# Dense products of a four-layer kernel: two tiles at a time, 712 columns as seven products of summed blocks

## The reference

```
x = x + x @ W0.T + 2 * sum_e gate_e * (x @ A_e.T) @ B_e.T     # 8 experts of rank 16, the two best by x @ Wr.T + bias
x = x + per batch: weights[condition].T @ x                   # mixes the 64 tokens of a batch
x = x + (x @ B2[adapter].T) @ A2[adapter].T                   # rank 16, one of 64 adapters for each batch
x = x + x @ W3.T + b3 + 2 * (x @ A3[slot]) @ B3[slot]         # rank 16, one of 32 slots for each batch
```

## Time and profile before

| | us |
|---|---|
| median of 3 runs (lowest to highest) | 938.36 (937.98 to 939.08) |
| the profiled execution | 938.59 |
| its span, first to last instruction | 936.8 |
| PE busy | 926.4 (99%) |
| DVE busy | 494.9 (53%) |
| ACT busy | 258.7 (28%) |
| POOL busy | 97.0 (10%) |

### The profile page before, as it was taken

How to read it: one execution, slowest core, us unless ns; L and a number is a source line. 1 busy time by engine, 2 the same in 40 slices (tenths; PEclk the granted TensorE clock), 3 DMA queues, 4 the chain that set the end, 5 groups by cost and what they waited for, 6 DMA issues and landing times.

```text
span 936.8 us, 14565 instructions
## 1 busy us (share of the span) xinstructions
PE 926.4 (99%) x4980; PEld 862.6 (92%) x4980; DVE 494.9 (53%) x1431; ACT 258.7 (28%) x526; POOL 97.0 (10%) x218
## 2 busy tenths in 40 slices
PE   8999999999999999999999999999999999999996
PEld 7888888888888899999999999999999999999996
DVE  6654444444333334565556555565655555565554
ACT  5544333333223222122212222221222122222211
POOL 1000110010000011011101111110111111011110
PEclk9999999999999999999999999999999999999999
DMA  7978776997676424655556465556556564655552
GB/s 246 313 257 267 222 250 220 317 327 224 205 231 188 142 83 115 186 155 163 165 161 177 138 185 154 174 145 179 159 159 168 157 185 131 189 158 166 156 166 94
DMA packets 93788, 175.10 MB, mean 187 GB/s; under 512 B 14609, under 2 KB 56978, under 8 KB 93714
## 3 DMA queue, kind: packets, MB, share of 16 engines
q1 hardware_dynamic: 93714, 174.17, 61.7%
HBM read 130.61 MB, written 49.81 MB: 193 GB/s over the span
## 4 chain that ended last, share of the span: by engine, by line
PE 98%; DMA 1%; DVE 0%; ACT 0%; issue 0%; SPq 0%; DVEq 0%
PE ps_y L886 46%; PE ps_o L861 27%; PE ps_v L861 9%; PE ps_o L898 5%; PE ps_y L892 5%; PE ps_o L985 2%; PE ps_v L922 1%; PE ps_o L958 1%; DMA chunk_a_raw<-mov 1%; PE ps_t L969 1%; PE ps_o L956 1%; PE ps_t L946 0%; PE ps_t L976 0%; PE ps_v L966 0%; DVE outb L846 0%
## 5 line engine op out<-in xcount | busy, mean ns | idle before, releaser
L886 PE MATMUL ps_y<-w_hi,x_hi 128*128 128x408 f32 x768 | 272.8, 355 | 0.0
L886 PE MATMUL ps_y<-w_hi,x_lo 128*128 128x408 f32 x768 | 267.4, 348 | 0.0
L886 PE MATMUL ps_y<-w_lo,x_hi 128*128 128x408 f32 x768 | 266.9, 348 | 0.0
L886 PEld LDWEIGHTS ps_y<-w_hi,x_hi 128*128 128x128 f32 x768 | 146.2, 190 | 1.9 <-issue 0.3
L886 PEld LDWEIGHTS ps_y<-w_hi,x_lo 128*128 128x128 f32 x768 | 144.4, 188 | 0.2
L886 PEld LDWEIGHTS ps_y<-w_lo,x_hi 128*128 128x128 f32 x768 | 144.2, 188 | 0.2
L658 DVE TENSOR_TENSOR stat_lo<-stat_raw,stat_hi 128x1024 fp32r<-128x1024 f32 (+1 forms) x63 | 75.0, 1191 | 24.3 <-ACT stat_hi L537 23.2
L861 PE MATMUL ps_o<-chunk_a_hi,stat_hi 128*128 128x512 f32 x216 | 84.5, 391 | 1.6 <-DVE chunk_a_lo L658 1.6
L861 PE MATMUL ps_o<-chunk_a_lo,stat_hi 128*128 128x512 f32 x216 | 84.1, 389 | 0.0
L861 PE MATMUL ps_o<-chunk_a_hi,stat_lo 128*128 128x512 f32 x216 | 84.0, 389 | 0.0
L658 DVE TENSOR_TENSOR y_lo<-ps_y,y_hi 128x408 fp32r<-128x408 f32 (+1 forms) x96 | 50.6, 536 | 57.1 <-ACT y_hi L537 57.1
(11 more groups left out here) (134 smaller groups left out, 1420.4 us busy)
## 6 DMA issues: line engine op xcount, KB each, us to landing
up<-tu SPq DMA_DIRECT2D x128, 256.0 KB, 5.0
stat_raw<-stat SPq DMA_DIRECT2D x59, 512.0 KB, 4.7
mdraw<-t SPq DMA_DIRECT2D x128, 208.0 KB, 2.9
x_raw<-x SPq DMA_DIRECT2D x32, 512.0 KB, 3.7
out<-outb SPq DMA_DIRECT2D x31, 512.0 KB, 5.1
t<-md_a SPq DMA_DIRECT2D x16, 576.0 KB, 6.8
chunk_a_raw<-mov SPq DMA_DIRECT2D x24, 256.0 KB, 5.8
tu<-rows_hi SPq DMA_DIRECT2D x24, 256.0 KB, 4.4
```

Of the source, the lines that this page charges most:

```text
L886: last = nc.tensor.matmul(ps_y[n][:, 0:YB], xT[par][a][:, k, :], w[c][:, k, Y[n]], start=k == 0 and m == 0, stop=k == KB - 1 and m == len( ...
```

## The change

Tiles are handled in pairs: a = 2j and b = 2j + 1, in 16 steps and one more. The 1024 columns of M are split: 312 (`PL`) stay an ordinary product, and with the 136 and 64 columns of the experts and adapters they make one product of 512 columns for each tile (`plain`, 24 matmuls). The other 712 are two halves of STRASSEN = 356 columns. For them the pair of tiles and M are 2 by 2 blocks: rows are tile a and tile b, inner blocks are the upper and the lower 512 features. Four sums of blocks of x (S1 to S4, made on POOL by `sums` for each pair) and four of M (T1 to T4, made on DVE once, in the last chunk of the table stage) allow seven products instead of eight (`winograd`, 12 matmuls of 356 columns each), in Winograd's form of Strassen's method. The products accumulate in PSUM where the form adds them, and ACT and DVE copy and add the partial results part1 and part2.

With it move: x is loaded a second time for the sums (`load_s2`, `load_s3`, `load_s4`), x and the sums lie in the places of the ring of stationary blocks and of the row buffers of the table stage; `ud_lo` goes from DVE to POOL; the high parts of the stacks go from DVE to ACT; the last chunk of the table stage makes M before the adapters' rows, and each group of rows for tu2 goes to it in four stores instead of two, for its columns now lie in two places. `mixed` waits for all three outputs of the tile before. The order of every engine's step is new. The diff, cut to its core:

```diff
+STRASSEN = 356
...
+    GROUPS += [(3, s) for s in U2_BLOCKS + [B0_BLOCK] + M0_BLOCKS]
+    GROUPS += [(4, s) for s in M0_BY_TWO + [B0_BLOCK] + U2_BLOCKS]
...
+    SH = STRASSEN
+    PL = D - 2 * SH
+    PH = PL // 2
...
+    MD_AT, P_AT, WCOLS = HL, HL + MD, HL + MD + PL
...
+    YE = (0, MD + PL, MD + PL + SH, YCOLS)
...
+            def load_x1(j):
+                if at(j, 0):
+                    sp.wait_ge(pe_group, G - 2)
+                else:
+                    sp.wait_ge(pe_p[3], j)
+                sp.dma_start(x1raw[:, :, :], x[2 * j + 1]).then_inc(ld_x1, 16)
...
+            def load_s3(j):
+                if at(j, 0):
+                    sp.wait_ge(st_rows[0], rows_stored(UNITS - 2))
+                else:
+                    sp.wait_ge(pe_p[6], j)
+                sp.dma_start(Sraw[2], x[2 * j][:, upper, :]).then_inc(ld_s[2], 16)
...
+            def step(j, front, back, fin):
+                a, b, a1, b1, b2 = 2 * j, 2 * j + 1, 2 * j - 2, 2 * j - 1, 2 * j - 3
+                if back:
+                    load_up(a1, chosen2.pop(a1), tu2, up2, pe_up2, ld_up2)
+                if front:
+                    load_md(b)
+                if fin:
+                    store_out(b2)
+                if back:
+                    load_up(a1, chosen3.pop(a1), tu3, up3, pe_out[2], ld_up3)
+                    load_mix(b1)
+                if front and not at(j, PAIRS - 1):
+                    load_x0(j + 1)
+                if back:
+                    load_up(b1, chosen2.pop(b1), tu2, up2, pe_up2, ld_up2)
+                    load_up(b1, chosen3.pop(b1), tu3, up3, pe_out[2], ld_up3)
+                if front and not at(j, PAIRS - 1):
+                    load_s2(j + 1)
+                    load_md(a + 2)
+                    load_s3(j + 1)
+                if back:
+                    store_out(a1)
+                if front and not at(j, 0):
+                    load_mix(a)
+                if front and not at(j, PAIRS - 1):
+                    load_x1(j + 1)
+                    load_s4(j + 1)
...
+            def sums(j):
+                def combine(dst, in0, in1, op):
+                    nc.gpsimd.tensor_tensor(out=dst, in0=in0, in1=in1, op=op).then_inc(pool_s, 1)
+                pool.wait_ge(ld_x1, 16 * (j + 1))
+                if at(j, 0):
+                    pool.wait_ge(pe_group, G - 1)
+                else:
+                    pool.wait_ge(pe_p[4], j)
+                combine(Sraw[0], x1raw[:, upper, :], x1raw[:, lower, :], ALU.add)
+                pool.wait_ge(ld_s[2], 16 * (j + 1))
+                combine(Sraw[2], Sraw[2], x1raw[:, upper, :], ALU.subtract)
+                pool.wait_ge(ld_s[1], 16 * (j + 1))
+                pool.wait_ge(pool_s, 4 * j + 1)
+                combine(Sraw[1], Sraw[0], Sraw[1], ALU.subtract)
+                pool.wait_ge(ld_s[3], 16 * (j + 1))
+                pool.wait_ge(pool_s, 4 * j + 3)
+                combine(Sraw[3], Sraw[3], Sraw[1], ALU.subtract)
...
+                if front:
+                    sums(j)
+                    place_w(b)
+                    ud_lo(b)
+                if back:
+                    mix_identity(b1)
+                if front:
+                    place_b(b)
+                    if not at(j, PAIRS - 1):
+                        place_w(a + 2)
+                        ud_lo(a + 2)
+                        place_b(a + 2)
+                    mix_identity(a)
...
+                        nc.vector.tensor_tensor(out=T3raw[:, n, :], in0=src[:, cols], in1=T3raw[:, n, :], op=ALU.subtract)
+                        dve.wait_ge(dve_t1, 2 * n + 2)
+                        nc.vector.tensor_tensor(out=T2raw[:, n, :], in0=src[:, cols], in1=T1raw[:, n, :],
+                                                op=ALU.subtract).then_inc(dve_ev, 1)
...
+                if front:
+                    x1_lo(j)
+                if back:
+                    h2_lo(a1)
+                if front:
+                    hidden_sum(a)
+                    gate(a)
+                    s_lo(j, 0)
+                    hidden_rows(a)
+                if back:
+                    h3_lo(a1)
+                if front:
+                    s_lo(j, 1)
+                    s_lo(j, 2)
+                if back:
+                    mix_lo(b1)
+                if front:
+                    s_lo(j, 3)
+                    if not at(j, PAIRS - 1):
+                        x0_lo(j + 1)
+                    hgT_lo(a)
+                    gate(b)
+                    plain_lo(a)
+                    hidden_sum(b)
+                if back:
+                    add_bias(a1)
+                if front:
+                    dve.wait_ge(pe_La, j + 1)
+                    dve.wait_ge(act_part, 3 * j + 1)
+                    nc.vector.tensor_tensor(out=yraw[0][:, YL], in0=ps_x[:, 0:SH], in1=part1[:, :],
+                                            op=ALU.add).then_inc(dve_La_raw, 1)
+                    hidden_rows(b)
+                    hgT_lo(b)
+                    dve.wait_ge(act_La, j + 1)
+                    rest(y[0][lo][:, YL], yraw[0][:, YL], y[0][hi][:, YL]).then_inc(dve_La, 1)
...
+            def plain(t, ks):
+                rows = x0 if t % 2 == 0 else x1
...
+                        last = nc.tensor.matmul(plain_bank(t)[:, 0:WCOLS], rows[a][:, k, :], w[c][:, k, :],
+                                                start=k == 0 and m == 0, stop=k == KB - 1 and m == len(PASSES) - 1,
+                                                skip_group_check=True)
...
+            def winograd(ps, rows, weights, first):
+                for k in range(HALF_KB):
+                    for m, (a, c) in enumerate(PASSES):
+                        last = nc.tensor.matmul(ps[:, 0:SH], rows[a][:, k, :], weights[c][:, k, :],
+                                                start=first and k == 0 and m == 0, stop=k == HALF_KB - 1 and m == len(PASSES) - 1,
+                                                skip_group_check=True)
+                return last
...
+                    pe.wait_ge(dve_x0, j + 1)
+                    pe.wait_ge(pool_md, a + 1)
+                    if at(j, 0):
...
+                        pe.wait_ge(dve_ev, M_DONE + 1)
...
+                        pe.wait_ge(dve_yp, b1 + 1)
+                    plain(a, range(0, 3))
+                if fin:
+                    h3_rows(b2)
+                if front:
+                    plain(a, range(3, 5))
+                if fin:
+                    ranks3(b2)
+                if front:
+                    plain(a, range(5, KB)).then_inc(pe_hl, 1)
+                    if at(j, 0):
...
+                    hidden_product(a)
+                if back:
+                    pe.wait_ge(dve_mix, a1 + 1)
+                    pe.wait_ge(dve_yp, a1 + 1)
+                    pe.wait_ge(dve_La, j)
+                    pe.wait_ge(dve_Ra, j)
+                    if fin:
+                        for n in range(3):
+                            pe.wait_ge(dve_out[n], a1)
+                    mixed(a1)
+                if front:
+                    if not at(j, 0):
+                        pe.wait_ge(dve_Lb, j)
+                    winograd(ps_w, A11, B11, True).then_inc(pe_p[0], 1)
+                if back:
+                    if front:
+                        pe.wait_ge(dve_vsum, 2 * a + 2)
+                    pe.wait_ge(dve_h2, a1 + 1)
+                    h2_rows(a1)
+                if front:
+                    if not at(j, 0):
+                        pe.wait_ge(dve_Rb_raw, j)
+                    winograd(ps_x, A12, B21, True).then_inc(pe_p[1], 1)
+                if back:
+                    ranks2(a1)
+                if front:
+                    repeated(a)
+                    pe.wait_ge(dve_x1, j + 1)
+                    pe.wait_ge(pool_md, b + 1)
+                    if not at(j, 0):
+                        pe.wait_ge(dve_Ra_raw, j)
+                    plain(b, range(0, HALF_KB))
+                if front:
+                    pe.wait_ge(dve_udb, a + 1)
+                if back:
+                    h3_rows(a1)
+                if front:
+                    plain(b, range(HALF_KB, KB)).then_inc(pe_hl, 1)
+                if back:
+                    ranks3(a1)
+                if front:
+                    gated_rows(a)
+                    if at(j, 0):
+                        pe.wait_ge(dve_t, HALF_KB)
+                    pe.wait_ge(act_part, 3 * j + 1)
+                    pe.wait_ge(dve_s, 4 * j + 3)
+                    winograd(ps_w, S[1], T2, False).then_inc(pe_p[5], 1)
+                    pe.wait_ge(dve_hgT, a + 1)
+                    pe.wait_ge(pool_mb, a + 1)
+                    experts(a, plain_bank(a)[:, HL:HALF], YP).then_inc(pe_xp, 1)
+                    experts(a, ps_x[:, 0:SH], YL).then_inc(pe_La, 1)
+                    hidden_product(b)
+                    pe.wait_ge(act_part, 3 * j + 2)
+                    winograd(ps_w, S[2], T3, False).then_inc(pe_p[6], 1)
```

(33 more changed lines are left out.)

858 lines of the change are left out of this document (506 added, 352 removed).

## The result

The changed kernel takes 932.68 us (median of five runs, 928.95 to 933.89) against 938.36 us: a ratio of 0.9935, 95% interval 0.9913 to 0.9957. It is faster, by 5.7 us where 20.4 were forecast.

The account below looks back on a forecast made before the run. TensorE's instruction time, priced by columns, was taken to bound the second stage. 340.7 + (925.5 - 340.7) - 36.7 + 2.6 - 3.2 + 4.2 + 2.0 + 22.0 = 916.4 us of span, 918.0 on the median; range 909 to 931.

Parts of the forecast that it names:

- Dense products: TensorE, second stage: 48 matmuls of 512 columns and 84 of 356 replace 144 of 408, saving 36.7 us over 16 pairs.
- rival C: Second-stage matmuls: weight loads set a floor of 188 ns, so narrow ones are not cheaper; 953 us, chance 0.03.
- TensorE's other work: Experts, mixing, rank and hidden products unchanged; two more late starts behind short matmuls in each pair, +2.6 us in all.
- the table stage: The 61 groups of 24 matmuls stay, VectorE's making of T1 to T4 is covered: 0, bounds 0 and +3 us.
- The sums: S1 to S4 on GpSimd in each pair: 1.29 us each, bounds 0.78 and 1.84, hidden by 0.9 us.
- rival B: GpSimd's sums set the pair through the hidden stack's wait: 2.1 us a pair at 1.84 a sum, 950 us, chance 0.06.
- The steady pair: Pairs of 34.6 us with no TensorE wait; h2T ready at +11.4, wanted at +12.1; bound +0.5 us a pair.
- The first pair: TensorE waits once, 4.2 us (bounds 0 and 8), for tile 1's selected rows, placed by GpSimd behind all four sums.
- The clock's share: First pair: the wait may cost the high clock level for the 24 matmuls behind it, 2 us, bounds 0 and 5.4.
- The tail: End of the kernel: three tiles left instead of one, each waiting for the one before; 22 us, bounds 18 and 24.
- Rival A: GpSimd and VectorE hold each other up in each pair: 0.3 to 0.9 us a pair, 923 to 932 us, chance 0.17.

Follow-up runs that it names:

- e4: Kernel after with the tile w allocated behind B11, B21, B22, 34176 bytes further in each partition: 930.61 us, ratio 0.991.
- e12: Kernel after with the tile w allocated between B11 and B21, 11392 bytes further in each partition: 932.77 us, ratio 0.9918.
- e11: Kernel after with e2, e4, e6, earlier mdraw and index reads in the first pair, and three more reorderings on ScalarE and VectorE: 920.46 us, ratio 0.9812.
- e10: Kernel after with the first of GpSimd's four sums in each pair done three times instead of once: 951.03 us, ratio 1.0132.
- e1: The kernel after run once more, unchanged, to size its spread: 934.71 us, ratio 0.9958.
- e5: Kernel after with mdraw of tile b loaded ahead of up in each step: 932.05 us, ratio 0.9922.
- e6: Kernel after with ScalarE's rounding of tile b's gathered rows moved behind the copy h2T, in pairs with a pair before: 931.77 us, ratio 0.9931.
- e7: Kernel after with mdraw of tile b issued behind the output store and the load of up3: 1021.96 us, ratio 1.0887.
- e2: Kernel after with the last tile's mixing matrix loaded ahead of the store and of up3, in the last step alone: 929.87 us, ratio 0.9912.

## Why the prediction was right or wrong

The saving on the products came for the most part. What failed is the cover of TensorE's waits: the prediction took no wait in a steady pair, because it left the transfer mdraw out of what stands ahead of h2T, and it sized the waits of the first pair and of the tail too small.

- *Dense products: right mechanism, a little too large.* Matmuls of 356 columns start 162.5 ns apart (161.7 forecast), so rival C is refuted. The Trainium skill (Perfetto Trace Analysis, Identifying the Most-Contended Engine) judges TensorE's headroom by MFU and by the busy share of weight loads. As a bound that share fails here: each of these loads lasts some 0.19 us and the matmuls still start every 0.162. The 512-column ones start 5.6 ns later each than in the table stage, where the prediction's bound was 2.1. (That bound was itself misread: its line gives 183.3 ns at 408 columns, not 183.7, so the excess of the earlier trace rows is 2.5.) Of the 5.6 the place of w makes 3.3, 2.6 us in all, recovered by e4 and e12. By these distances the products save some 31 us, my estimate, where 36.7 were forecast; the pair as a whole is only 0.2 us longer than forecast, since the rest of it costs less.
- *TensorE's other work, the table stage: right.* Without any wait a steady pair is 34.65 us in e11, against 34.6. The table stage ends at 339.65 (340.7 forecast).
- *The sums: right.* 1.28 to 1.30 us alone (1.29 forecast), 1.42 and 1.35 in the mean. Their cover was about right as well: e10 lengthened the chain by 2.6 us and lost 1.4 a pair, where the forecast's covers give 1.0 and rival B's sum 2.5.
- *The steady pair: wrong, in the step that lists what stands ahead of h2T.* The list held the stacks, the gate, the exponential and the roundings, but took the data of the roundings as there. The selected rows of tile b are issued behind up and behind 2.5 us of index reads, at +4.1, and land at +10.3 to +12.7. The prediction followed the queue of SyncE for the next tile's rows and not for these. The time that it found for h2T, +11.4, fits the chain that it listed: without its idle 0.41 us ScalarE would have been done at about +11.3. In the undisturbed pair the transfer adds only those 0.41 us, within the cover of 0.6; in others it lands up to 2.4 us later and TensorE waits. e1, e5, e6 and e7 show it from four sides. Of the loss, though, this link and the mix on ScalarE behind it hold only 1.4 to 6.2 us together, depending on the execution.
- *The first pair: right mechanism, too small.* 4.2 us of wait were forecast and 1.68 + 4.74 came; the cause of the longer one was SyncE's order and the index reads (mdraw issued at +9.25, landed at +14.9), not the fourth sum, which was done at +11.8 (+12.8 forecast). The clock's share, 1.5 us by the 24 matmuls (7.07 against 5.60), was put at 2.0. In the eight profiles that leave the first pair's order as it was (after, e1, e2, e4 to e7, e12) it takes 37.6 to 39.9 us; after, at 38.5, is below five of the others.
- *The tail: right mechanism, mis-sized.* 22.0 forecast, 25.7 measured. Each tile waits for the one before, as forecast. The term of 1.3 us for the load of up3 should have been one for the mix behind it (2.7 us by e2), and the low clock over the mixing matmuls was left out.
- *Rival A: in part.* In the first pair VectorE and GpSimd hold each other up: 2.23 us for 1.22, 2.06 for 1.30, 0.72 for 0.18. The Trainium skill (SBUF — State Buffer, on the port diagram) has an exclusive lock between GpSimd and VectorE, which the one that starts first holds for its whole instruction; the trace agrees, for the rest of x1 ends 1.08 us behind the third sum and vparts ends with the fourth. In a steady pair such meetings land where there is cover: gsel takes 1.36 us instead of 0.48, and the pair is 34.81 or 34.65 with no wait. A wait of TensorE behind one was seen only in the first pair.
- *The sum of the gap.* From 918.0 to 932.7 are 14.7 us: first pair 3.2 to 4.6, address of w 2.6, tail 3.7, late rows and mix in steady pairs 1.4 to 6.2; the profile of after has the low ends of these, its sum is 10.8 us. e11 takes most of them away and stands at 920.5. Open is what differs between executions in runs that have no trace: e6's other three runs are 1.3 to 3.0 us over its profiled one.
